# Causal mask of the key-on-partition scores in sixteen quarter-height passes, four side by side

## The chip, the cores and the metric

The kernel runs on one core of a Trainium2 chip. The metric is the device time of one execution in microseconds. Five engines work side by side on their own instruction lists: TensorE (matmuls, and a unit beside it that loads their weights), VectorE, ScalarE, GpSimd and SyncE, which issues most transfers. They wait for one another by semaphores.

## The reference

Two decoder layers over x of shape (32, 128, 128): 32 batches of 128 positions with 128 channels. Cut to the order of the parts:

```python
x = x + _L0_attn_ref(_layernorm(x), ...)           # 16 heads of 8, rotary
x = x + _L0_xattn_ref(_layernorm(x), ctx_768, ...) # 16 heads of 8, clipped
x = x + _L0_ffn_ref(_layernorm(x), ...)
x = x + _L1_attn_ref(_layernorm(x), ...)           # the causal one
x = x + _L1_xattn_ref(ctx_768, _layernorm(x), mask_BxS2_bk0, ...)
x = x + _L1_ffn_ref(_layernorm(x), ...)            # 8 experts, 2 per token
```

The part that the change touches is the causal attention of the second layer:

```python
att = jnp.einsum('bhqd,bhkd->bhqk', q, k) * scale
causal = jnp.tril(jnp.ones((Tx, Tx), dtype=bool))
att = jnp.where(causal[None, None], att, -jnp.inf)
att = jax.nn.softmax(att, axis=-1)
y = jnp.einsum('bhqk,bhkd->bhqd', att, v)
```

## The kernel before

The kernel is a row of phases, each a block of its own: self and cross attention of layer 0 in one block, a guard, the feed-forward of layer 0, the causal attention, the latent cross attention, the expert feed-forward. A phase starts when the one before it has ended. The attention phases all come from `attention` (line 225 on), which is called once for self and cross and once for the causal kind.

A phase works through 32 batches (n), in groups (G) of 4. P is 128, U is 4, GB is 4, GT is 512 (one bank of the accumulation memory). The 16 heads stand in 4 units (u) of 4 heads (j); a unit's 32 channels lie on partitions 32u to 32u + 31 (`rows_of`). PSUM is split by hand: `S` has two banks, `T` four, `OM` and `PB` one each.

For each batch scores are made twice. `scores` (lines 382 to 394) makes them with the query on the partition into `S`, two units at a time (`pair`), for the row maxima that VectorE takes (line 591, `maxes`). `key_scores` (from line 396) makes them again with the key on the partition into `T`, one bank per unit, in three rounds of four matmuls of 32 rows and 512 columns: high parts times high parts (line 408), then the query's low part (411), then the key's (413). `shift` (425) subtracts the maxima, ScalarE exponentiates (521), `weigh` (452) multiplies with the values and with ones.

In the causal kind `hide` (lines 370 to 380) first writes the mask into the banks by matmuls of constants: a slice of the mask table as weights and a slice of the identity, repeated for the 4 heads, as the moving operand. It takes two banks. Bank i uses partitions 64i to 64i + 63, so that two passes can run side by side, and each pass covers 64 of the 128 columns of each head, 4 x 64 = 256 columns. Two banks take 2 x 2 passes. `scores` calls it once per pair with table 0, `key_scores` twice with table 1, for banks 0 and 1 and for banks 2 and 3: 8 passes. The tables lie in the constants `const_r` (name `cr`), which are loaded at the start of the program (line 124) and copied by ScalarE (line 162).

What follows what on an engine is written out by hand in `ORDERS`. TensorE's list for the causal kind is "s0 k^5 T m y f0 s1 x^6 f1 w q^5 v^4". Iteration n runs the scores of batch n + 2 (s0, s1), the key scores of batch n (T), the transposed maxima of n + 1 (m), the output projection of n - 2 (y), the shift of n (f0, f1) and the weighing of n - 1 (w). A step with ^ runs once per group, so many batches before the group's first: the key projection k of a group stands between s0 and T, 5 iterations ahead.

Of the kernel before, what the change touches and what calls it, by code (L numbers as in the profile page):

```python
# [19 lines left out]
P = 128  # L20
# [4 lines left out]
GT = GB * P  # L25
E0 = 8
W_FFN0 = 3 * (E0 // 2 + 1) * P + E0
U = 4
# [35 lines left out]


C_ID, C_ONES, C_MASK = 0, P, 5 * P
C_PAIR = C_MASK + 4 * P
C_BEFORE = C_PAIR + (E0 // 2) * P
C_FULL = C_BEFORE + P
N_CONST_R = C_FULL + P  # L70
# [152 lines left out]
def attention(nc, phase, kinds, sb, bank, context=None, x_ready=None):  # L223
# [5 lines left out]
    def kind(n):  # L229
        return kinds[n // B]  # L230
# [16 lines left out]
    cr = sb["const_r"]  # L247
# [13 lines left out]
    S, T = bank[:, 0:2 * GT], bank[:, 2 * GT:6 * GT]  # L261
    OM, PB = bank[:, 6 * GT:7 * GT], bank[:, 7 * GT:8 * GT]

    def s_bank(u):
        return S[:, (u % 2) * GT:(u % 2 + 1) * GT].rearrange("p (j k) -> p j k", j=U)

    def t_bank(u):
        return T[:, u * GT:(u + 1) * GT]
# [35 lines left out]
    with ExitStack() as ctx:  # L304
# [48 lines left out]
        def rows_of(u):  # L353
            return slice(32 * u, 32 * u + 32)

        def batch_cols(n):
            return slice((n % GB) * P, (n % GB + 1) * P)
# [6 lines left out]
        def _(pe):  # L364
# [2 lines left out]
                pe.matmul(out, l[0], r[1], start=False, stop=False)  # L367
                return pe.matmul(out, l[1], r[0], start=False, stop=True)

            def hide(banks, c):  # L370

                half = P // 2
                for part in range(2):
                    at = C_MASK + (2 * c + part) * P
                    for i, out in enumerate(banks):
                        mine = slice(i * half, (i + 1) * half)
                        pe.matmul(out.rearrange("p (j q) -> p j q", j=U)[:, :, part * half:(part + 1) * half],
                                  cr[mine, at:at + P],
                                  cr[mine, C_ID + i * half:C_ID + (i + 1) * half].unsqueeze(1).broadcast_to([half, U, half]),
                                  start=part == 0, stop=False)  # L380

            def scores(n, pair):
                causal = kind(n) == "causal"
                if pair == 0:
                    pe.wait_ge(k_masked, n + 1)
                if 2 * n + pair > 0:
                    pe.wait_ge(max_done, 2 * n + pair)
                units = (2 * pair, 2 * pair + 1)
                if causal:
                    hide([S[:, u * GT:(u + 1) * GT] for u in range(2)], 0)  # L390
                for u in units:
                    mm = pe.matmul(s_bank(u), kq_hi[QUERY][(n // GB) % 2][rows_of(u), batch_cols(n)],  # L392
                                   k_hi_m[n % 2][rows_of(u), :, :], start=not causal, stop=True)
                mm.then_inc(scored, 1)

            def key_scores(n):
                causal, clip = kind(n) == "causal", kind(n) == "cross"
                pe.wait_ge(q_masked, 2 * n + 2)
                if n > 0:
                    pe.wait_ge(exp_done, 2 * n)  # L400
                g = (n // GB) % 2
                k_hi, k_lo, q_hi, q_lo = kq_hi[KEY][g], kq_lo[KEY][g], q_hi_m[n % 2], q_lo_m[n % 2]
                if causal:
                    for u in (0, 2):
                        hide([t_bank(u), t_bank(u + 1)], 1)
                out = [t_bank(u).rearrange("p (j q) -> p j q", j=U) for u in range(U)]
                for u in range(U):
                    pe.matmul(out[u], k_hi[rows_of(u), batch_cols(n)], q_hi[rows_of(u), :, :],
                              start=not causal, stop=False)
                for u in range(U):  # L410
                    pe.matmul(out[u], k_hi[rows_of(u), batch_cols(n)], q_lo[rows_of(u), :, :], start=False, stop=False)
                for u in range(U):
                    mm = pe.matmul(out[u], k_lo[rows_of(u), batch_cols(n)], q_hi[rows_of(u), :, :],  # L413
                                   start=False, stop=clip)
                    if clip and u % 2 == 1:
                        mm.then_inc(keyed, 1)
# [78 lines left out]
            for step, i in steps("PE"):  # L495
                if step == "T":
                    key_scores(i)
                elif step in ("f0", "f1"):
                    shift(i, int(step[1]))
                elif step == "y":  # L500
                    out_project(i)
                elif step in ("s0", "s1"):
                    scores(i, int(step[1]))
                elif step == "m":
                    transpose_max(i)
                elif step == "w":
                    weigh(i)
                elif step == "x":
                    transpose_x(i)
                elif step == "c":  # L510
                    transpose_c(i)
                else:
                    project(step, i)
# [362 lines left out]
def gated_experts(nc, phase, sb, ps, ready):  # L876
# [12 lines left out]
    with ExitStack() as ctx:  # L889
# [59 lines left out]
        def _(pe):  # L949
# [22 lines left out]
            def spread_gate(it, n, k):  # L972
                if k == 0:
                    pe.wait_ge(g_done, it * 2 + (n + 1))
                if (NB - 1) * n + k > 0:
                    pe.wait_ge(gate_copied, it * (2 * NB - 2) + ((NB - 1) * n + k))
                sel = cr[0:2 * E0, C_PAIR + k * P:C_PAIR + (k + 1) * P]
                pe.matmul(GATE[:, :], sel, g_parts[n % 2][:, :], start=True, stop=True).then_inc(gate_spread, 1)
# [1326 lines left out]
def shape_constants():  # L2305

    c = np.zeros((P, N_CONST), np.float32)
    eye = np.eye(P, dtype=np.float32)
    c[:, C_ID:C_ID + P] = eye
    for u in range(U):  # L2310
        c[32 * u:32 * u + 32, C_ONES + u * P:C_ONES + (u + 1) * P] = 1.0
        for g in range(U):
            c[32 * u + g, C_DIAG + g] = 1.0
            c[32 * u + DH * g:32 * u + DH * (g + 1), C_SLOT + g] = 1.0
    e = np.arange(E0)
    c[:, C_EARLIER:C_EARLIER + E0 * E0] = (e[None, :] < e[:, None]).astype(np.float32).reshape(1, -1)
    for h in range(2):
        c[h * P // 2:(h + 1) * P // 2, C_HEAD + h] = 1.0
    c[:, C_BEFORE:C_BEFORE + P] = np.triu(np.ones((P, P), np.float32), 1)
    c[:, C_FULL:C_FULL + P] = 1.0  # L2320
    c[:, C_DESCEND:C_DESCEND + E1] = E1 - np.arange(E1)
    c[:, C_FILL:C_FILL + MOST] = TT * np.arange(MOST)
    c[:, C_REGION:C_REGION + E1] = B * P * np.arange(E1)
    c[:, C_TILE:C_TILE + N_TILES] = np.arange(N_TILES)
    c[:, C_TILE_ROW:C_TILE_ROW + N_TILES] = TT * np.arange(N_TILES) - B * P
    c[:, C_HOME:C_HOME + 2 * B] = P * np.arange(2 * B)[None, :] + np.arange(P)[:, None]
    for k in range(E0 // 2):
        c[[2 * k, E0 + 2 * k], C_PAIR + k * P:C_PAIR + k * P + P // 2] = 1.0
        c[[2 * k + 1, E0 + 2 * k + 1], C_PAIR + k * P + P // 2:C_PAIR + (k + 1) * P] = 1.0
    hidden = np.triu(np.ones((P, P), np.float32), 1) * np.float32(MASKED)  # L2330
    for n, table in enumerate((hidden.T, hidden)):
        for half in range(2):
            rows = table[half * P // 2:(half + 1) * P // 2]
            at = C_MASK + (2 * n + half) * P
            c[0:P // 2, at:at + P] = rows
            c[P // 2:P, at:at + P] = rows
    rate = (np.float32(1.0) / np.float32(10000.0) ** (np.arange(0, DH, 2, dtype=np.float32) / np.float32(DH)))
    ch = np.arange(D)

    angle = (rate[ch % (DH // 2)][:, None] * np.arange(P, dtype=np.float32)[None, :]).astype(np.float32)  # L2340
    sign = np.where(ch % DH < DH // 2, -1, 1).astype(np.float32)[:, None]
    c[:, C_ROPE:C_ROPE + P] = np.cos(angle)
    c[:, C_ROPE + P:C_ROPE + 2 * P] = sign * np.sin(angle)

    angle = (rate[ch % DH // 2] * (ch // DH).astype(np.float32)).astype(np.float32)
    sign = np.where(ch % 2 == 0, -1, 1).astype(np.float32)
    for n, table in enumerate((np.cos(angle), sign * np.sin(angle))):
        c[:, C_TURN + n * P:C_TURN + (n + 1) * P] = table[None, :]
        c[:, C_TURN_COL + n] = table
    return c  # L2350


def packed(i):
# [36 lines left out]
    def experts(routed, shared):  # L2390
# [13 lines left out]
        "cols": np.stack(cols, 1),  # L2404
        "rows": np.concatenate([rows_of(r) for r in rows], 1),
        "consts": shape_constants(),
    }

# [15 lines left out]
```

## Time and profile before

| | |
|---|---|
| median of 3 runs | 1434.62 us (1428.91 to 1439.69) |
| the profiled execution | 1435.96 us |
| its span | 1434.2 us |
| granted TensorE clock, mean | 0.912 |
| TensorE matmuls busy | 1197.7 us (84%) |
| VectorE, ScalarE, GpSimd busy | 878.1, 674.8, 768.1 us |
| mask passes (line 377) | 512, from 715.8 to 957.0 us |

The span is the time from the first to the last instruction of the profiled execution; the time has a little around it. Times of rows are in us from the start of the span unless marked ns. PE is TensorE's matmuls, PEld its weight loads, DVE VectorE, ACT ScalarE, POOL GpSimd. Matmuls are pipelined: a row's length holds its latency, so what a round costs is read from the starts of two rounds.

### The profile page before, as it was taken

To read this page: it belongs to the slowest core of one execution; us is meant where nothing else is said; L and a number is where in the kernel's file an instruction comes from. 1 tells how busy PE (TensorE), PEld (TensorE's weight loads), DVE (VectorE), ACT (ScalarE), POOL (GpSimd) and SP (SyncE) were. 2 spreads that over 40 slices of the span, in tenths; PEclk is the share of its full clock that TensorE was granted. 3 is DMA by queue.
4 is the path that set the end of the run, shared out by engine and by line. 5 is a ranking of instruction groups with operands and counts; after the bars stand their busy time and mean duration, and the time that the engine had idled before them with its cause. 6 is when DMAs were issued, how large, how long until landed. Compare 5 with 4: busy or idle time off the path is not lost. (4 is left out here: it accounts for less than half of the span.)

```text
span 1434.2 us, 33962 instructions
## 1 busy us (share of the span) xinstructions
PE 1197.7 (84%) x12478; PEld 901.5 (63%) x12478; DVE 878.1 (61%) x2007; ACT 674.8 (47%) x1298; POOL 768.1 (54%) x870
## 2 busy tenths in 40 slices
PE   1899998788888874999799999984999993199992
PEld 0577775555555563666467777764899983088881
DVE  3688876599999955666255666555888843122223
ACT  1345444344545422455345545437888631055551
POOL 3777873555666511444455555525776757344452
PEclk9999998799999985999789999996999955599996
DMA  9910000000000000000000000000000001256656
GB/s 346 380 56 10 2 2 15 14 15 15 14 15 7 2 2 1 1 1 0 1 2 2 2 2 3 2 2 23 12 13 2 20 25 52 78 192 201 196 192 179
DMA packets 58863, 75.27 MB, mean 52 GB/s; under 512 B 13246, under 2 KB 40003, under 8 KB 58576
## 3 DMA queue, kind: packets, MB, share of 16 engines
q1 hardware_dynamic: 53328, 63.59, 13.8%
q0 software_dynamic: 4544, 8.47, 1.7%
q8 instruction: 101, 1.65, 0.5%
q10 hardware_dynamic: 832, 1.09, 0.2%
q14 instruction: 58, 0.48, 0.1%
HBM read 40.24 MB, written 31.70 MB: 50 GB/s over the span
## 5 line engine op out<-in xcount | busy, mean ns | idle before, releaser
L591 DVE TENSOR_REDUCE maxes<-bank 128x8 f32<-128x1024 f32 x192 | 234.4, 1221 | 56.6 <-PE bank L392 55.1
L521 ACT ACTIVATE self_probs<-bank 128x1024 f32<-128x1024 f32 x128 | 129.1, 1022 | 46.1 <-PE bank L425 45.7
L1429 POOL DMA_INDIRECT returned<-relu_y,relu_slots x78 | 76.7, 984 | 93.8 <-DVE relu_y L1404 81.3
L1372 ACT ACTIVATE relu_hidden<-bank,cols 128x256 f32<-128x256 f32 x156 | 74.0, 474 | 94.0 <-PE bank L1330 80.5
L528 ACT ACTIVATE self_neg_max<-bank 128x512 fp32r<-128x512 f32 x64 | 38.2, 597 | 149.9 <-PE bank L439 149.9
L732 POOL TENSOR_TENSOR self_k_hi_m<-self_kq_hi,const 128x512 fp32r<-128x512 f32 x64 | 66.6, 1041 | 78.4 <-ACT self_kq_hi L549 78.4
L1330 PE MATMUL bank<-relu_s,relu_w_tile 128*128 128x256 f32 x312 | 94.3, 385 | 0.5 <-DVE relu_s L1398 0.5
L1338 PE MATMUL bank<-relu_hidden,relu_w_tile 128*128 128x256 f32 x312 | 92.5, 379 | 0.0
L1398 DVE COPY relu_s<-bank 128x256 f32<-128x256 f32 x39 | 16.6, 425 | 110.5 <-issue 81.1
L597 DVE TENSOR_SCALAR bank<-bank 128x1024 f32<-128x1024 f32 x64 | 78.2, 1223 | 3.3 <-PE bank L413 3.3
L601 DVE RECIPROCAL self_recip<-bank 128x128 f32<-128x128 f32 x64 | 61.2, 957 | 30.2 <-PE bank L452 28.2
L2215 POOL DMA_INDIRECT routed<-latent_rows,latent_place_i x64 | 63.0, 984 | 30.8 <-issue 16.6
L732 POOL TENSOR_TENSOR causal_q_lo_m<-causal_kq_lo,const 128x512 fp32r<-128x512 f32 x32 | 33.3, 1041 | 84.5 <-PE bank L425 84.4
L452 PE MATMUL bank<-self_probs,values 128*32 128x128 f32 x2048 | 73.1, 286 | 1.4 <-ACT self_neg_max L528 1.2
L452 PE MATMUL bank<-self_probs,head_ones 128*32 128x128 f32 x2048 | 70.8, 280 | 0.0
L425 PE MATMUL bank<-self_neg_max,const_r 32*128 32x512 f32 x256 | 62.0, 475 | 9.7 <-DVE bank L597 6.3
L521 ACT ACTIVATE causal_probs<-bank 128x1024 f32<-128x1024 f32 x64 | 64.5, 1022 | 5.2 <-PE bank L425 2.7
L732 POOL TENSOR_TENSOR self_q_lo_m<-self_kq_lo,const 128x512 fp32r<-128x512 f32 x64 | 66.7, 1042 | 0.3 <-PE bank L425 0.2
L732 POOL TENSOR_TENSOR self_q_hi_m<-self_kq_hi,const 128x512 fp32r<-128x512 f32 x64 | 66.6, 1041 | 0.0
L452 PEld LDWEIGHTS bank<-self_probs,values 128*32 128x32 f32 x2048 | 54.9, 113 | 18.6 <-issue 15.9
L439 PE MATMUL bank<-ident,maxes 128*128 128x128 f32 x384 | 65.2, 294 | 0.5 <-POOL maxes L755 0.3
L1338 PEld LDWEIGHTS bank<-relu_hidden,relu_w_tile 128*128 128x128 f32 x312 | 59.3, 190 | 8.3 <-ACT relu_hidden L1372 0.2
(380 smaller groups left out, 3434.9 us busy)
## 6 DMA issues: line engine op xcount, KB each, us to landing
relu_w_tile<-in_w_ffn SPq DMA_DIRECT2D x39, 512.0 KB
routed<-blank SPq DMA_DIRECT2D x1, 19760.0 KB, 60.9
relu_slots<-routed SPq DMA_DIRECT2D x39, 130.0 KB
relu_back<-returned SPq DMA_DIRECT2D x16, 256.0 KB, 4.4
x_all<-in_x SPq DMA_DIRECT2D x8, 256.0 KB, 8.2
x_before<-x_all SPq DMA_DIRECT2D x8, 256.0 KB, 2.7
out_x<-x_all SPq DMA_DIRECT2D x8, 256.0 KB, 4.0
self_ctx_in<-in_ctx SPq DMA_DIRECT2D x8, 192.0 KB, 2.6
```

Of the source, the lines that this page charges most:

```text
L425: mm = pe.matmul(t_bank(u), cr[rows_of(u), C_ONES + u * P:C_ONES + (u + 1) * P], neg_max[n % 2][rows_of(u), :], start=False, stop=True, sk ...
L439: mm = pe.transpose(OM[:, j * P:(j + 1) * P], maxes[n % 2][:, j * P:(j + 1) * P], sb["ident"][:, :])
L452: mm = pe.matmul(OM[rows_of(u), c:c + P], of(u, j), probs[n % 2][:, u, j, :], start=j == 0, stop=j == U - 1)
L521: act.activation(probs[n % 2][:, 2 * pair:2 * pair + 2, :, :].rearrange("p u j q -> p (u j q)"), T[:, 2 * pair * GT:(2 * pair + 2) * GT], ...
L591: dve.tensor_reduce(out.rearrange("p j u -> p u j"), S.rearrange("p (u j k) -> p u j k", u=2, j=U), AX.X, ALU.max, negate=True).then_inc(m ...
L597: dve.tensor_scalar(t, t, CLAMP / scale, -CLAMP / scale, ALU.min, ALU.max).then_inc(clipped, 1)
L732: pool.tensor_tensor(out[n % 2][:, :, :], src[(n // GB) % 2][:, batch_cols(n)].bitcast(F32).unsqueeze(1).broadcast_to([P, U, P]), slots.un ...
L1330: pe.matmul(HT[i % 2][:, 0:TT], w_tile[t % NW][:, c * P:(c + 1) * P], s[t % 2][:, :], start=True, stop=True)\
L1338: pe.matmul(YT[t % 2][:, 0:TT], w_tile[t % NW][:, F1 + c * P:F1 + (c + 1) * P], hidden[i % C1][:, :], start=c == 0, stop=c == C1 - 1).then ...
L1372: act.activation(hidden[i % C1][:, :], HT[i % 2][:, 0:TT], ACT.Relu, bias=sb["cols"][:, bass.ds(r + (COL_RELU + c), 1)]).then_inc(hidden_d ...
L1429: pool.indirect_dma_start(returned[:, :], bass.IndirectOffsetOnAxis(ap=slots[t % NX][:, b, P:P + 1].bitcast(I32), axis=0), y[t % NY][:, b, ...
L2215: pool.indirect_dma_start(routed[:, :], bass.IndirectOffsetOnAxis(ap=place_i[u % 3][:, k, b:b + 1], axis=0), rows[G % 4][:, k, n % GB, :], ...
```

## The change

`hide` takes a list of banks of any length and the place of the table, and splits partitions and columns by the number of banks. `scores` calls it as before, with two banks. `key_scores` calls it once with all four banks of `T`: 4 x 4 = 16 passes of 32 rows and 4 x 32 = 128 columns, bank i on partitions 32i to 32i + 31. The table of the key scores gets four parts instead of two, each repeated on four groups of partitions, so the constants grow by 2 x 128 columns.

```diff
-C_PAIR = C_MASK + 4 * P
+C_PAIR = C_MASK + 6 * P
...
-            def hide(banks, c):
-
-                half = P // 2
-                for part in range(2):
-                    at = C_MASK + (2 * c + part) * P
+            def hide(banks, mask):
+
+                share = P // len(banks)
+                for part in range(len(banks)):
+                    at = mask + part * P
                     for i, out in enumerate(banks):
-                        mine = slice(i * half, (i + 1) * half)
-                        pe.matmul(out.rearrange("p (j q) -> p j q", j=U)[:, :, part * half:(part + 1) * half],
+                        mine = slice(i * share, (i + 1) * share)
+                        pe.matmul(out.rearrange("p (j q) -> p j q", j=U)[:, :, part * share:(part + 1) * share],
                                   cr[mine, at:at + P],
-                                  cr[mine, C_ID + i * half:C_ID + (i + 1) * half].unsqueeze(1).broadcast_to([half, U, half]),
-                                  start=part == 0, stop=False)
+                                  cr[mine, C_ID + i * share:C_ID + (i + 1) * share].unsqueeze(1)
+                                  .broadcast_to([share, U, share]), start=part == 0, stop=False)
...
-                    hide([S[:, u * GT:(u + 1) * GT] for u in range(2)], 0)
+                    hide([S[:, u * GT:(u + 1) * GT] for u in range(2)], C_MASK)
...
-                    for u in (0, 2):
-                        hide([t_bank(u), t_bank(u + 1)], 1)
+                    hide([t_bank(u) for u in range(U)], C_MASK + 2 * P)
...
-    for n, table in enumerate((hidden.T, hidden)):
-        for half in range(2):
-            rows = table[half * P // 2:(half + 1) * P // 2]
-            at = C_MASK + (2 * n + half) * P
-            c[0:P // 2, at:at + P] = rows
-            c[P // 2:P, at:at + P] = rows
+    at = C_MASK
+    for table, parts in ((hidden.T, 2), (hidden, 4)):
+        share = P // parts
+        for part in range(parts):
+            for i in range(parts):
+                c[i * share:(i + 1) * share, at:at + P] = table[part * share:(part + 1) * share]
+            at += P
```

On TensorE, an iteration with a key projection between scores and mask. Before (outputs are named with the partition count of the bank, x8 is the number of passes in a row):

```order
L377 MATMUL bank<-const_r 128x4x64 x4
L392 MATMUL bank<-causal_k_hi_m,causal_kq_hi 128x512 x2
L366 MATMUL bank<-causal_x_hi,w_hi 128x512
L367 MATMUL bank<-causal_x_lo,w_hi 128x512
L368 MATMUL bank<-causal_x_hi,w_lo 128x512
L377 MATMUL bank<-const_r 128x4x64 x8
L408 MATMUL bank<-causal_q_hi_m,causal_kq_hi 128x512 x4
L411 MATMUL bank<-causal_q_lo_m,causal_kq_hi 128x512 x4
L413 MATMUL bank<-causal_q_hi_m,causal_kq_lo 128x512 x4
L439 MATMUL bank<-ident,maxes 128x128 x4
```

The same place of the changed kernel, whose lines behind `hide` stand one higher:

```order
L377 MATMUL bank<-const_r 128x4x64 x4
L392 MATMUL bank<-causal_k_hi_m,causal_kq_hi 128x512 x2
L366 MATMUL bank<-causal_x_hi,w_hi 128x512
L367 MATMUL bank<-causal_x_lo,w_hi 128x512
L368 MATMUL bank<-causal_x_hi,w_lo 128x512
L377 MATMUL bank<-const_r 128x4x32 x16
L407 MATMUL bank<-causal_q_hi_m,causal_kq_hi 128x512 x4
L410 MATMUL bank<-causal_q_lo_m,causal_kq_hi 128x512 x4
L412 MATMUL bank<-causal_q_hi_m,causal_kq_lo 128x512 x4
L438 MATMUL bank<-ident,maxes 128x128 x4
```

On TensorE again, an iteration without a key projection, from the weighing of the iteration before on. Before:

```order
L452 MATMUL bank<-causal_probs,head_ones 32x128 x16
L377 MATMUL bank<-const_r 128x4x64 x4
L392 MATMUL bank<-causal_k_hi_m,causal_kq_hi 128x512 x2
L377 MATMUL bank<-const_r 128x4x64 x8
L408 MATMUL bank<-causal_q_hi_m,causal_kq_hi 128x512 x4
L411 MATMUL bank<-causal_q_lo_m,causal_kq_hi 128x512 x4
L413 MATMUL bank<-causal_q_hi_m,causal_kq_lo 128x512 x4
L439 MATMUL bank<-ident,maxes 128x128 x4
```

The same place of the changed kernel:

```order
L451 MATMUL bank<-causal_probs,head_ones 32x128 x16
L377 MATMUL bank<-const_r 128x4x64 x4
L392 MATMUL bank<-causal_k_hi_m,causal_kq_hi 128x512 x2
L377 MATMUL bank<-const_r 128x4x32 x16
L407 MATMUL bank<-causal_q_hi_m,causal_kq_hi 128x512 x4
L410 MATMUL bank<-causal_q_lo_m,causal_kq_hi 128x512 x4
L412 MATMUL bank<-causal_q_hi_m,causal_kq_lo 128x512 x4
L438 MATMUL bank<-ident,maxes 128x128 x4
```

Nothing changes places in either; the 8 passes ahead of the first key-score round have become 16. In the second place the mask stands right behind the scores of line 392, in the first behind the key projection (lines 366 to 368).

## Rows read from the trace of the kernel before

**Rows 1.** Stretches: length, busy PE, PEld, DVE, ACT, POOL, granted clock, DMA share, GB/s
```profile
727.00:966.00 239.00, 235.38 (x3509) 165.53 (x3508) 138.63 (x238) 112.16 (x152) 125.92 (x134) 1.00 0.01 2
966.00:1000.00 34.00, 14.48 (x60) 12.24 (x61) 16.31 (x76) 24.56 (x57) 18.04 (x35) 0.60 0.10 24
```

**Rows 2.** Waits of PE from 727 to 966 us: us in total, times, longest
```profile
PE bank L465 <- DVE causal_o_t L605: 1.4, 1, 1.4
...
PE bank L377 <- ACT causal_probs L521: 0.2, 1, 0.2
```

**Rows 3.** Timeline of PE, one batch: start, length, line, rows*weight columns, moving operand, count
```profile
849.25 0.50 PE L392 MATMUL bank<-causal_k_hi_m,causal_kq_hi 32*128 32x512 f32 x2
849.68 0.74 PE L377 MATMUL bank<-const_r 64*128 64x256 f32 x8
850.35 0.51 PE L408 MATMUL bank<-causal_q_hi_m,causal_kq_hi 32*128 32x512 f32 x4
850.68 0.41 PE L411 MATMUL bank<-causal_q_lo_m,causal_kq_hi 32*128 32x512 f32 x4
850.91 0.42 PE L413 MATMUL bank<-causal_q_hi_m,causal_kq_lo 32*128 32x512 f32 x4
```

**Rows 4.** Timeline of PEld, same batch; then the group, 740 to 955 us
```profile
849.68 0.54 PEld L377 LDWEIGHTS bank<-const_r 64*128 64x128 f32 x8 [0.24 <-issue]
...
850.46 0.20 PEld L411 LDWEIGHTS bank<-causal_q_lo_m,causal_kq_hi 32*128 32x128 f32 x4
850.69 0.20 PEld L413 LDWEIGHTS bank<-causal_q_hi_m,causal_kq_lo 32*128 32x128 f32 x4
...
L377 PEld LDWEIGHTS bank<-const_r 64*128 64x128 f32 x456 | 32.2, 185 | 20.4 <-issue 18.7 <-POOL causal_q_hi_m L732 1.2
```

**Rows 5.** Timeline of PE, further on in the same iteration
```profile
852.50 0.50 PE L377 MATMUL bank<-const_r 64*128 64x256 f32 x4
852.93 0.49 PE L392 MATMUL bank<-causal_k_hi_m,causal_kq_hi 32*128 32x512 f32 x2
853.26 0.40 PE L425 MATMUL bank<-causal_neg_max,const_r 32*128 32x512 f32 x2
853.59 1.08 PE L452 MATMUL bank<-causal_probs,values 128*32 128x128 f32 x32
854.49 1.06 PE L452 MATMUL bank<-causal_probs,head_ones 128*32 128x128 f32 x32
```

**Rows 6.** Timeline of PE, latent attention: full height, 128 and 256 columns
```profile
1061.91 0.22 PE L1724 MATMUL bank<-latent_mask_rows,const_r 128*128 128x128 f32 x1
1061.97 0.34 PE L1722 MATMUL bank<-latent_k_hi,latent_q_hi 128*128 128x256 f32 x1
1062.14 0.22 PE L1724 MATMUL bank<-latent_mask_rows,const_r 128*128 128x128 f32 x1
```

**Rows 7.** Timeline of PE, value projection: full height, 128 columns
```profile
856.53 0.27 PE L366 MATMUL bank<-w_hi,causal_x_hi 128*128 128x128 f32 x1
856.64 0.27 PE L367 MATMUL bank<-w_lo,causal_x_hi 128*128 128x128 f32 x1
```

**Rows 8.** Timeline of PE, a batch with the key projection ahead of the mask
```profile
842.13 0.74 PE L377 MATMUL bank<-const_r 64*128 64x256 f32 x8
...
843.14 0.40 PE L411 MATMUL bank<-causal_q_lo_m,causal_kq_hi 32*128 32x512 f32 x4
```

**Rows 9.** Page, part 2 (GB/s in 40 slices), and timeline of the start
```profile
GB/s 346 380 56 10 2 2 15 14 15 15 14 15 7 2 2 1 1 1 0 1 2 2 2 2 3 2 2 23 12 13 2 20 25 52 78 192 201 196 192 179
...
7.09 1.80 ACT L162 ACTIVATE const_r<-staged_consts 128x1920 fp32r<-128x1920 f32 x1 [2.36 <-DMA staged_consts<-in_consts]
...
13.05 0.29 DVE L178 TENSOR_TENSOR staged_weights<-staged_weights,const 128x128 f32<-128x128 f32 x1 [13.05 <-DMA w_out<-in_weights]
```

**Rows 10.** Timeline of ACT and DVE, the batch of rows 3
```profile
847.59 1.02 ACT L521 ACTIVATE causal_probs<-bank 128x1024 f32<-128x1024 f32 x1
...
849.79 1.23 DVE L591 TENSOR_REDUCE maxes<-bank 128x8 f32<-128x1024 f32 x1 [0.45 <-PE bank L392]
```

## Prediction

> **What bounds the kernel now.** I read the busy time by stretch first, then the waits of the stage that the change touches, then its order of time, one batch at a time. The causal attention's steady part runs from about 727 to 966 us [rows 1]: TensorE's matmuls are busy 235.38 of 239.00 us there at a granted clock of 1.00 (2.4 GHz), while VectorE has 138.63, ScalarE 112.16 and GpSimd 125.92. After 966 the stage is over and the clock at 0.60. TensorE hardly waits for anybody: the longest wait in those 239 us is 1.4 us, once [rows 2]. So this stage lasts as long as TensorE's own list, and what is cut from the list comes off the end as long as nothing else turns up as a wait.
>
> But busy does not mean streaming. In one batch [rows 3] the two score matmuls of 512 columns start at 849.25 and the eight mask passes only at 849.68, 0.43 us later; the first key scores start at 850.35 and the second round at 850.68, 0.33 later; the third comes 0.23 behind that. All three are rounds of 512 columns that differ in what stands around them. 0.23 is the price where the weights come ahead: the loads of the second and third rounds start while the round before still streams (850.46 against 850.68, 850.69 against 850.91) [rows 3, 4]. 0.33 is that and 0.10 for a first load that nobody could take ahead. 0.43 is that and another 0.10, in which the array runs empty before the next load may start: the mask's loads begin at 849.68 with 0.24 us of idle load unit before them, put down to issue and to no engine [rows 4]. What distinguishes 0.43 is that the number of rows changes, 32 to 64 [rows 3]. Where 32 rows follow 32 rows, at 852.93 and 853.26, the step is 0.33 and no drain shows [rows 5]. So a change between full, half and quarter height costs about 0.10 of drain and 0.10 of exposed load: 0.20 us.
>
> Could it be another shape that costs, and not another height? Then the quarter-height mask of 128 columns would still drain ahead of and behind the key scores of 512, and nothing would be gained. The nearest rows are full-height neighbours of 256, 128 and 256 columns, which follow one another without a drain, 0.06 and 0.17 us apart [rows 6]; so I take the height. By the height the sum is -11.0 us, by the shape it is 0.
>
> On this the Trainium skill has a rule, in TensorEngine Tiling (Array Packing), Key Properties: going to another tiling mode drains the array, going to another tile of the same mode does not. By that rule the sum is the one by the height.
>
> **The change, part by part.** Every causal batch runs the mask before its key scores once, 32 batches.
>
> 1. *Passes.* Before: 8 passes of 64 rows and 256 columns, in 4 rounds of two side by side. After: 16 passes of 32 rows and 128 columns, in 4 rounds of four. Streaming halves. But a round also loads 128 weight columns per pass, and these loads are as long as before. The eight loads of the old block take 0.54 us as a group, and the mean of one is 0.185, so three steps from round to round take 0.355 and one 0.118 [rows 4]. Two full-height neighbours with 128 columns and 128 weight columns go at 0.11 [rows 7]. A stream of 128 columns whose weights are there takes only 0.06: 1061.91 to 1061.97 [rows 6]. So a new round is bound by its load: 0.11 at the least. I take 0.118, as the new block's loads start at the same point as the old, once the last matmul of their row group has begun. Halving the columns is worth nothing by itself; four rounds stay four rounds.
>
> 2. *Will four loads at once hold that pace?* The old block had two. Four quarter-height loads stand ahead of every key-score round, and the round at 850.35 costs the same 0.33 with four loads exposed [rows 3] as the one at 852.93 with two [rows 5]: the loads run side by side. The issue of 16 pairs of load and matmul is bounded by the weighing, where 32 pairs take 0.90 us, 853.59 to 854.49 [rows 5], so 16 take 0.45. Four rounds at 0.118 are 0.47, just above it. The mask operands are constants, so no new wait comes with the extra passes.
>
> 3. *Height changes.* The mask now has the height of the key scores behind it and, mostly, of the scores ahead of it.
>  - Scores right ahead: before, scores to second key round is 850.68 - 849.25 = 1.43 us [rows 3]. After: 0.33 (as from the first to the second key round, its own load exposed), four rounds 0.47, then the first key round with weights loaded ahead, 0.23. Together 1.03, so 0.40 saved.
>  - Something of full height ahead (key projection or weighing): before, mask to second key round is 843.14 - 842.13 = 1.01 [rows 8]. After: 0.22 for the first round with its load exposed (0.10 + 0.118), two rounds 0.24, one more step 0.12 to the key scores, 0.23. Together 0.81, so 0.20 saved.
>  By the list of orders the key projection of groups 2 to 7 stands between scores and mask (6 batches), and the last 2 batches have no scores two batches on. In 1 more, the second, the mask waits 0.2 us for the exponential [rows 2], so only 0.20 is saved. So 23 x 0.40 + 9 x 0.20 = 9.2 + 1.8 = 11.0 us. With rounds of 0.11 it would be 32 x 4 x 0.008 = 1.0 more.
>
> 4. *The scores' own mask* (two banks, half height, 4 passes per pair) stays, with its changes of height.
>
> 5. *The constants* grow from 1920 to 2176 columns, 128 KB more. At the first slice's 346 GB/s [rows 9] that is 0.37 us. VectorE's first work waits for loads until 13.05 us [rows 9] and the first projection hangs on it, so I count it in full; the lower end is 0. ScalarE's copy of 1.80 us ends at 8.89 [rows 9] and grows by 256/1920 of that, 0.24 us; ScalarE is idle until its first normalisation, so that costs nothing, and would cost 0.24 if it did.
>
> 6. *Who becomes late next.* The second score mask must wait for VectorE's maximum of the first: that ends at 849.79 + 1.23 = 851.02, the mask starts at 852.50 [rows 5, 10]. Of these 1.48 us at most 0.42 go. The key mask waits for the exponential that ends at 847.59 + 1.02 = 848.61 [rows 10] and starts at 849.68, 1.07 later; nothing between them gets shorter. So TensorE remains the bound.
>
> Sum: -11.0 + 0.4 = -10.6 us. Against the profiled execution (span 1434.2, time 1435.96) that gives 1425.4 us; its time is 1.3 above the median of 1434.62, and from the median the sum gives **1424.0 us**, 0.7% less.
>
> **Rivals.**
> - *Weights don't come ahead in quarter rounds* (chance 0.12). Then a round is load plus stream, 0.118 + 0.057. Adds 0.057 x 4 x 32 = 7.3 us: 1431.3. For it: no row shows rounds this short at quarter height with 128 weight columns. Against it: the key rounds load the same four row groups during the stream before [rows 4]. The Trainium skill, TensorE: Matmul & The Clock Gate, Part 3, says that a load overlaps running matmuls only where its row group is another one, which taken strictly is this rival; the loads at 850.46 and 850.69 go against it.
> - *Slower: the four loads queue for one path* (0.03). 4 x 0.11 = 0.44 per round, (0.44 - 0.118) x 4 x 32 = 41 us more: 1465. It decides from a round of 0.118 + 10.6 / 128 = 0.20 us on. Against it: 0.33 with four loads and with two, as above.
> - *No gain* (0.08): the drains stay because they hang on the shape, or VectorE's maxima, the GpSimd masks or the exponentials become the bound: 1434 to 1436. For it: these engines are 47 to 58% busy in long pieces of 1.0 to 1.2 us. Against it: the neighbours without a drain [rows 6] and the slack of 1.07 and 1.48 us.
> - *More than counted* (0.07): rounds of 0.11 and a stage end that falls better with the clock, which goes to 0.60 in the 34 us behind the stage [rows 1]; a stretch at the lower level costs up to half of its length. About 1419.
>
> **How the numbers follow.** The forecast has 0.70, its own range being 1420 to 1428: the sum within a microsecond or so, and the spread of single runs, which here go from 1428.91 to 1439.69. The range from 1416 to 1432 takes in the load rival and most of the case of more than counted. About 1% is what a measurement of this kernel can tell from no change, and faster by over 1% means below 1420.3. The forecast reaches there by its spread in about 2 of 9 cases (0.15), more than counted mostly (0.05), together 0.20. Slower by over 1% is the queue rival, 0.03, and a little of the third, 0.04 in all. The rest, 0.76, is within 1%.
>
> **What the new profile would show.** Scores to mask 0.33 instead of 0.43; mask to key scores about 0.47 instead of 0.67; first to second key round 0.23 instead of 0.33; the load unit's idle pieces ahead of the key mask gone in 23 batches; the stage near 11 us shorter with TensorE as full as now. If mask to key scores is 0.70, the first rival holds; if it is over 1 us, the second. If these steps are right and the stage isn't shorter, a wait of TensorE for another engine must have come up. The sum is wrong in its height changes if mask to key scores still shows idle load time ahead of the key round.

## The result

The changed kernel takes 1425.26 us in the median of 8 executions (1420.62 to 1430.07), the kernel before 1435.54 in 8 (1428.91 to 1445.33): a ratio of 0.9925, interval 0.9907 to 0.9944. That is 10.3 us less, by the interval 8 to 13. Forecast were 10.6 less from a median of 1434.62, so 1424.0 us.

From the page of the changed kernel, span and the first row of part 1:

```profile
span 1420.8 us, 34474 instructions
...
PE 1192.8 (84%) x12734; PEld 904.7 (64%) x12734; DVE 877.0 (62%) x2007; ACT 675.0 (48%) x1298; POOL 767.3 (54%) x870
```

The counts say that 256 more matmuls run, each with its load: 16 instead of 8 passes in 32 batches. TensorE is busy for 1192.8 us instead of 1197.7, which is no measure of the gain.

The steady part of the causal attention, busy time by stretch (columns as in [rows 1]), and TensorE's waits in it:

```profile
727.00:955.00 228.00, 225.59 (x3714) 164.79 (x3712) 138.36 (x236) 113.95 (x155) 126.67 (x135) 0.99 0.01 2
```

```profile
PE bank L377 <- DVE maxes L590: 0.5, 1, 0.5
```

TensorE is as full as before (225.59 of 228.00 us), VectorE, ScalarE and GpSimd do the same work in less time, and TensorE's longest wait is 0.5 us. No other engine has taken over.

How long the stage is I read from the first to the last start of the mask passes, with the clock's lower level for the first 11 us of it in both. Before:

```profile
L377 PE MATMUL bank<-const_r x512: 271/278/579, 715.8 to 957.0; 64*128 64x256 f32 x171
```

After:

```profile
L377 PE MATMUL bank<-const_r x768: 216/273/579, 720.2 to 949.8; 32*128 32x128 f32 x128, 64*128 64x256 f32 x64
```

241.2 us before, 229.6 after: 11.6 less. From the first normalisation of the stage (`causal_mean_var`) to that of the next it is 268.7 and 257.1, the same 11.6. The stage's period is sharper still, as nothing but TensorE sets it. The transposes of x run once per group of four batches; starts of two neighbours before and after:

```profile
776.13 0.66 PE L472 MATMUL bank<-ident,causal_xn 128*128 128x128 f32 x4
...
806.80 0.66 PE L472 MATMUL bank<-ident,causal_xn 128*128 128x128 f32 x4
```

```profile
777.88 0.65 PE L471 MATMUL bank<-ident,causal_xn 128*128 128x128 f32 x4
...
807.04 0.66 PE L471 MATMUL bank<-ident,causal_xn 128*128 128x128 f32 x4
```

30.67 us before, 29.16 after, and the same to 0.03 for the five such pairs of a trace that lie at full clock. The two at the stage's start, where the clock is low and not every step runs yet, are shorter. The change takes 1.51 us off four batches.

**One batch after**, scores right ahead of the mask (columns as in [rows 3]):

```profile
760.27 0.49 PE L392 MATMUL bank<-causal_k_hi_m,causal_kq_hi 32*128 32x512 f32 x2
760.29 0.77 PE L377 MATMUL bank<-const_r 32*128 32x128 f32 x14
760.78 0.45 PE L407 MATMUL bank<-causal_q_hi_m,causal_kq_hi 32*128 32x512 f32 x2
760.89 0.27 PE L377 MATMUL bank<-const_r 32*128 32x128 f32 x2
761.00 0.44 PE L407 MATMUL bank<-causal_q_hi_m,causal_kq_hi 32*128 32x512 f32 x2
761.07 0.61 PE L410 MATMUL bank<-causal_q_lo_m,causal_kq_hi 32*128 32x512 f32 x4
...
761.84 0.33 PE L438 MATMUL bank<-ident,maxes 128*128 128x128 f32 x1
```

and of the load unit:

```profile
760.29 0.62 PEld L377 LDWEIGHTS bank<-const_r 32*128 32x128 f32 x14
...
761.84 0.20 PEld L438 LDWEIGHTS bank<-ident,maxes 128*128 128x128 f32 x2 [0.36 <-issue]
```

The mask starts 0.01 to 0.02 us behind the scores, not 0.33: the two row groups that the scores of this pair leave idle begin their passes at once. From there on the row groups run apart, two ahead, two behind: mask passes (760.89) come after the first key scores of other row groups (760.78). The loads of the mask begin at 760.29 too, beside the scores, and run on to 760.91. The end is the transposed maximum at 761.84, with 0.36 us of idle load unit ahead of it, the change back to full height. From the scores to it: 1.57 us. Before, the scores of [rows 3] at 849.25 were followed by

```profile
851.26 0.55 PE L439 MATMUL bank<-ident,maxes 128*128 128x128 f32 x3
```

2.01 us. So 0.44 saved.

**A batch with the key projection ahead**, after:

```profile
753.37 0.67 PE L377 MATMUL bank<-const_r 32*128 32x128 f32 x16
753.87 0.46 PE L407 MATMUL bank<-causal_q_hi_m,causal_kq_hi 32*128 32x512 f32 x4
754.15 0.41 PE L410 MATMUL bank<-causal_q_lo_m,causal_kq_hi 32*128 32x512 f32 x4
...
754.73 0.33 PE L438 MATMUL bank<-ident,maxes 128*128 128x128 f32 x1
```

1.36 us from mask to transposed maximum. Before, the mask of [rows 8] at 842.13 was followed by

```profile
843.70 0.55 PE L439 MATMUL bank<-ident,maxes 128*128 128x128 f32 x3
```

1.57 us, so 0.21 saved. Three of the one and one of the other make 1.53; the period gives 1.51. Of the 32 batches of the trace 23 are of the first kind, and in just these the load unit's idle time ahead of the key mask is gone; 9 are of the second kind, as counted.

### The profile page after: what moved, and what is told of

It is laid out like the page before. It is cut to its first block and busy times, and to the rows that moved or that the text cites. A ratio compares the mean times of both kernels' runs of the same rounds, so it can differ in the third digit from the quotient of the medians.

```text
span 1420.8 us, 34474 instructions
## 1 busy us (share of the span) xinstructions
PE 1192.8 (84%) x12734; PEld 904.7 (64%) x12734; DVE 877.0 (62%) x2007; ACT 675.0 (48%) x1298; POOL 767.3 (54%) x870
```

## Experiments

All periods below are read from the starts of the transposes as above; "stage" is the time from the first to the last mask pass. Kernels without a ratio ran once, so their whole time says little; period and stage are what they are read by.

| kernel | period of 4 batches, us | stage, us | whole kernel against before |
|---|---|---|---|
| before | 30.67 | 241.2 | |
| changed | 29.16 | 229.7 | 0.9925 (0.9907 to 0.9944) |
| changed, again | 29.16 | 229.7 | 0.9933 (0.9903 to 0.9964) |
| a_wide | 29.23 | 230.4 | |
| b_narrow | 32.12 | 252.9 | |
| c_by_bank | 29.59 | 232.9 | |
| e_same | 29.57 | 232.8 | |
| e_height | 30.79 | 242.2 | |
| v_second | 27.53 | 220.4 | 0.9895 (0.9822 to 0.9968) |
| v_second again | 27.53 | 220.4 | 0.9881 (0.9834 to 0.9928) |
| v_both | 27.57 | 227.8 | 0.9920 (0.9895 to 0.9946) |
| v_late | 27.53 | 218.3 | 0.9869 (0.9835 to 0.9903) |

### Is it the streaming or the height? (a_wide, b_narrow)

a_wide keeps quarter height and makes each pass 256 columns wide again:

```diff
+                for part in range(4):
+                    at, half, shift = mask + part * P, part // 2 * 64, (1 - part % 2) * 32
...
+                        pe.matmul(out.rearrange("p (j q) -> p j q", j=U)[:, :, half:half + 64],
+                                  cr[mine, at:at + P],
+                                  cr[mine, C_WIDE + shift:C_WIDE + shift + 64].unsqueeze(1)
+                                  .broadcast_to([32, U, 64]), start=part == 0, stop=False)
```

> The changed kernel with passes of quarter height that are 256 columns wide again (16 passes, four side by side, a moving operand padded with zeros, same result). Read by the time from the first to the last mask pass, 241.2 us before and 229.6 us after the change. Theory (the gain is the removed changes of height, a round is bound by its weight load of 0.11 to 0.12 us): a stream of 256 columns takes 0.11 and hides behind the load, so 229 to 231 us. Rival (the gain is the halved streaming): all of it is lost, about 241 us.

Mask and key scores of a batch with the key projection ahead:

```profile
845.93 0.75 PE L388 MATMUL bank<-const_r 32*128 32x256 f32 x16
846.52 0.40 PE L418 MATMUL bank<-causal_q_hi_m,causal_kq_hi 32*128 32x512 f32 x4
846.74 0.40 PE L421 MATMUL bank<-causal_q_lo_m,causal_kq_hi 32*128 32x512 f32 x4
```

The stage takes 230.4 us, the period is 29.23 instead of 29.16. Twice the columns cost 0.07 us per four batches. So the halved streaming is worth next to nothing, as expected.

b_narrow is the other half: the kernel before, its half-height passes 128 columns wide and twice as many.

```diff
-                    for u in (0, 2):
-                        hide([t_bank(u), t_bank(u + 1)], 1)
+                    for u in (0, 2):
+                        hide_narrow([t_bank(u), t_bank(u + 1)], 1)
```

with, in `hide_narrow`, parts of 32 columns per head and `cr[mine, q:q + 32]` as the moving operand.

> The kernel before with its half-height mask of the key scores in passes of 128 columns: 16 passes, two side by side, 8 rounds; each pass streams half as much, the heights and their changes stay. Theory (a round costs its weight load, however few columns it streams): 4 more rounds of 0.11 to 0.118 us in 32 batches, 14 to 15 us more than the kernel before: 255 to 256 us from first to last mask pass. Rival (rounds cost their streaming): 8 rounds of half the columns cost what 4 did, 241 us.

```profile
853.84 1.11 PE L389 MATMUL bank<-const_r 64*128 64x128 f32 x16
854.87 0.50 PE L420 MATMUL bank<-causal_q_hi_m,causal_kq_hi 32*128 32x512 f32 x4
```

1.03 us from mask to key scores instead of 0.67, the stage 252.9 instead of 241.2, 11.7 more. The rival had it at 241. The expectation of 14 to 15 more was somewhat high: the four further rounds cost 0.36 together, 0.09 each. Taken one by one the later rounds start 0.11 us apart (six steps from 854.00 to 854.67), the price of a load. The rest of the difference stands in the first step, 0.17 us where the kernel before has 0.23 (849.68 to 849.90): its stream is half as long. The two runs together leave the removed changes of height, and what they let the row groups do, as what the change gains by.

### The price of a change of height by itself (e_same, e_height)

Both add one pass with zero weights between mask and key scores, in every batch; e_same on 32 rows, e_height on 64:

```diff
+                    pe.matmul(T[:, 0:P], cr[0:P // 2, C_WIDE:C_WIDE + P], cr[0:P // 2, C_ID:C_ID + P],
+                              start=False, stop=False)
```

(`P // 4` in e_same.)

> The changed kernel with one more pass between mask and key scores: quarter height, 128 columns, zero weights, into bank 0 (adds zero). It has the height of its neighbours. Both theories: one load-bound round more on row group 0 in 32 batches, 0.118 x 32 = 3.8 us, so 233.5 us from first to last mask pass (229.7 without it).

> The same extra pass at half height (64 rows, same columns, zero weights), so that the height changes twice between mask and key scores. Theory of the height: drain 0.10, load 0.11, stream 0.06, drain 0.10, and the key round's load 0.11 exposed, about 0.47 us in each of 32 batches: 15 us, 244.5 us from first to last mask pass, 11 us above the run with the quarter-height pass. Rival (what costs is another shape of the moving operand or the number of passes, not the height): the same 233.5 us as that run.

e_same, a batch with the key projection ahead:

```profile
848.53 0.67 PE L378 MATMUL bank<-const_r 32*128 32x128 f32 x16
849.03 0.27 PE L406 MATMUL bank<-const_r 32*128 32x128 f32 x1
849.04 0.55 PE L410 MATMUL bank<-causal_q_hi_m,causal_kq_hi 32*128 32x512 f32 x4
849.32 0.50 PE L413 MATMUL bank<-causal_q_lo_m,causal_kq_hi 32*128 32x512 f32 x4
```

e_height, the same place:

```profile
853.03 0.67 PE L378 MATMUL bank<-const_r 32*128 32x128 f32 x16
853.63 0.32 PE L406 MATMUL bank<-const_r 64*128 64x128 f32 x1
853.88 0.51 PE L410 MATMUL bank<-causal_q_hi_m,causal_kq_hi 32*128 32x512 f32 x4
854.22 0.41 PE L413 MATMUL bank<-causal_q_lo_m,causal_kq_hi 32*128 32x512 f32 x4
```

From mask to the second key round it is 0.79 us with the quarter-height pass and 1.19 with the half-height one. Per batch, from the periods, the quarter-height pass costs (29.57 - 29.16) / 4 = 0.10 us and the half-height pass (30.79 - 29.16) / 4 = 0.41. The 0.30 between them are two changes of height at the same place, with the same columns and weights. That is 0.15 per change, drain and exposed load together, somewhat less than the 0.20 of the prediction. One thing comes with the height: in e_same three of the four key scores start beside the extra pass (849.04), in e_height none can, so the 0.15 holds this loss too. The stages are 232.8 us, where 233.5 had been expected, and 242.2, where the theory of the height had 244.5 and the rival 233.5. One pass of the wrong height in a batch takes back the whole gain of the change (0.41 against 0.38 us per batch).

### How far the row groups run apart (c_by_bank)

```diff
+                for i, out in enumerate(banks):
+                    for part in range(4):
```

instead of parts outside and banks inside.

> The changed kernel with the 16 passes in another order: all four parts of bank 0 (row group 0), then of bank 1, and so on, instead of part by part over the banks. Same passes, same result. If matmuls start strictly in program order, the row groups work one after another: 16 steps of about 0.118 us instead of 4, 1.42 us more in each of 32 batches, some 45 us more, 275 us from first to last mask pass. If a row group goes ahead of a waiting one (as the passes of the idle row groups seem to do right behind the scores in the trace after), the time stays near 229.6 us.

```profile
852.40 0.50 PE L401 MATMUL bank<-causal_k_hi_m,causal_kq_hi 32*128 32x512 f32 x2
852.74 0.58 PE L386 MATMUL bank<-const_r 32*128 32x128 f32 x13
853.13 0.44 PE L416 MATMUL bank<-causal_q_hi_m,causal_kq_hi 32*128 32x512 f32 x1
853.13 0.30 PE L386 MATMUL bank<-const_r 32*128 32x128 f32 x3
853.25 0.47 PE L416 MATMUL bank<-causal_q_hi_m,causal_kq_hi 32*128 32x512 f32 x3
```

The stage is 232.9 us: 3.2 more, not 45. So a matmul does not wait for earlier ones of another row group to finish; in a batch with the key projection ahead the block costs the same 0.50 us in either order:

```profile
845.48 0.70 PE L386 MATMUL bank<-const_r 32*128 32x128 f32 x16
845.98 0.48 PE L416 MATMUL bank<-causal_q_hi_m,causal_kq_hi 32*128 32x512 f32 x4
...
846.86 0.33 PE L447 MATMUL bank<-ident,maxes 128*128 128x128 f32 x1
```

But going ahead has an end. Behind the scores the mask begins 0.34 us later, not 0.01. In the order by parts the idle row groups' first passes stand third and fourth in the list, here ninth and thirteenth, and they don't start early. The place in the list alone doesn't explain it. In the batch with the key projection ahead, the window 845.48 to 845.60 shows four passes, one for each row group:

```profile
845.48 0.36 PE L386 MATMUL bank<-const_r 32*128 32x128 f32 x4
```

All four start by 845.52, and the others only from 845.65 on. So the first pass of row group 3, the thirteenth in the list, goes ahead of nine that wait. What differs behind the scores is that row group 0 has four passes waiting behind a running matmul, and not three. Whether that is the limit wasn't tried.

The run also says how much of the gain hangs on the order. From scores to transposed maximum it is now 1.71 us (the scores of 852.40, and below), against 1.57 by parts and 2.01 before:

```profile
854.11 0.33 PE L447 MATMUL bank<-ident,maxes 128*128 128x128 f32 x1
```

So 0.30 of the 0.44 us come with the equal height in this order too, and 0.14 only when the passes are listed by parts. With the key projection ahead it is 1.38 against 1.36. Three of 0.14 and one of 0.02 make 0.44, and the periods differ by 0.43. The loads fit: by parts loads of mask passes go on beside the scores (from 760.29), by banks a single one is taken ahead (852.51) and the next starts at 852.74.

### Further versions (v_second, v_both, v_late)

v_second makes the mask of the second pair of scores in quarter height too, on row groups 2 and 3, between the two halves of the shift:

```diff
-                    hide([S[:, u * GT:(u + 1) * GT] for u in range(2)], C_MASK)
+                    if pair:
+                        hide_quarter([S[:, u * GT:(u + 1) * GT] for u in range(2)], C_MASK + 6 * P, 2)
+                    else:
+                        hide([S[:, u * GT:(u + 1) * GT] for u in range(2)], C_MASK)
```

> A version that goes further: the mask of the second pair of scores is also made in quarter-height passes (2 banks, 4 rounds of two, on row groups 2 and 3), while the first pair keeps half height. Between the first half of the shift (row groups 0 and 1) and the second half there is then no change of height. Before, these steps are 0.43 + 0.43 + 0.33 = 1.19 us. If a row group can go ahead while others stream, the mask rounds run beside the shift and the whole takes about 0.79 us: 0.40 less in 31 batches, 12 us, 217 us from first to last mask pass and about 1413 us. If the mask waits for the shift's streams, 0.33 + 0.47 + 0.23 = 1.03: 5 us less, 225 us and 1420 us.

```profile
845.65 0.50 PE L437 MATMUL bank<-causal_neg_max,const_r 32*128 32x512 f32 x2
845.66 0.66 PE L387 MATMUL bank<-const_r 32*128 32x128 f32 x8
846.16 0.45 PE L405 MATMUL bank<-causal_k_hi_m,causal_kq_hi 32*128 32x512 f32 x2
846.44 0.41 PE L437 MATMUL bank<-causal_neg_max,const_r 32*128 32x512 f32 x2
```

From shift through mask and scores to the second half of the shift: 0.79 us instead of 1.19 (852.07 to 853.26 before), the mask starting 0.01 behind the shift. The period falls by 1.63 us to 27.53, which is 0.41 per batch. But the stage took 220.4 us, not 217, and the whole kernel 0.9895, hardly below the changed kernel and with a wide interval. What the stage lacks stands at its start. The stretches at the lower level there (columns as in [rows 1], the granted clock third from last), first the changed kernel's, then v_second's:

```profile
706.90:730.80 23.90, 16.10 (x57) 10.57 (x57) 7.10 (x17) 8.57 (x17) 13.75 (x17) 0.50 0.00 0
```

```profile
712.80:743.50 30.70, 23.04 (x108) 15.48 (x109) 10.71 (x27) 9.50 (x18) 16.19 (x20) 0.50 0.00 1
```

The clock is at 0.50, its lower level (1.2 GHz), and before and behind them at 1.00. The stretch begins 0.9 to 1.3 us behind the stage's first normalisation in every profile. In the profile before, both of the changed kernel and those of a_wide, b_narrow, c_by_bank, e_same and e_height, the lower level at the stage's start lasted 23.9 us. In v_second it lasted 30.7. The form of the key mask is not what moves it, as it is the same before and after the change.

In the whole kernel more is in play than the stage. In the profiled execution of v_second the feed-forward ahead of the stage, whose code is the same, took 183.0 us, in that of the changed kernel 175.6.

v_both uses `hide_quarter` for both pairs.

> Quarter-height mask for both pairs of scores. The second pair gains as in v_second (0.40 us per batch, 12 us less than the changed kernel without the clock's share). The first pair stands behind work of full height: its mask takes 4 rounds instead of 2 (0.57 to the scores instead of 0.43), but the scores' load comes ahead (0.23 instead of 0.33 behind them): +0.03 us per batch if the key mask starts as before, 1 us more than v_second, 218 us from first to last mask pass. If the key mask of row groups 2 and 3 goes ahead beside the first pair's mask, it is even with v_second or up to 0.2 us per batch better (6 us), 211 us.

> The changed kernel once more, unchanged, on the same chip as v_both and in turns with the kernel before: 229.7 us from first to last mask pass if the clock stands as in its first profile, ratio 0.9925 within its interval.

The changed kernel gave 229.7 us and a ratio of 0.9933 again. v_both has the same period as v_second, 27.57, so the first pair neither gains nor loses; the overlap hoped for there is not to be seen. And its clock rose later still, after 47.8 us:

```profile
714.90:762.70 47.80, 39.91 (x280) 29.67 (x282) 16.48 (x36) 18.01 (x30) 26.20 (x31) 0.50 0.00 1
```

Its stage took 227.8 us and the kernel 0.9920, the same as the changed kernel. 218 or 211 us had been expected for the stage: most of what the shorter period brings is given back by the clock at the start.

v_late is v_second with the old form for the scores of the first four batches:

```diff
-                    if pair:
+                    if pair and n > 3:
```

> v_second with the scores' masks of the first four batches in the form of the changed kernel (half height), so that the start of the stage, where TensorE's clock still stands at its lower level, has the same work as in the changed kernel. In the first profile of v_second the lower level lasted 30.7 us there, in v_both 47.8, in the changed kernel 23.9 both times. If the new form of the masks at the start is what holds the clock down, the lower level lasts 23.9 us again and the time from first to last mask pass is 229.7 - 28 x 0.41 = 218.2 us, some 11.5 us below the changed kernel: about 1414 us, ratio 0.984. If the length of that stretch is chance, it varies here too, and v_late and v_second are alike. The period of four batches is 27.5 us in either case.

> v_second unchanged, in turns with v_late. If the masks' form holds the clock down: the lower level at the start of the stage lasts about 30 us again and the kernel is 2 to 4 us slower than v_late. If it is chance: the same time as v_late within the spread of single runs.

v_late's stretch at the lower level:

```profile
706.00:729.90 23.90, 16.31 (x57) 10.61 (x57) 7.11 (x17) 8.78 (x17) 13.63 (x16) 0.50 0.00 0
```

The lower level lasted 23.9 us again, and the stage took 218.3 us where 218.2 had been expected. v_second's lasted 30.7 again, its stage 220.4 again. So the length of that stretch repeats with the form of the first masks and is not chance. Why TensorE's clock comes later with quarter-height masks there isn't settled: the passes there are more, shorter and less high, and no run separates these. In whole kernels v_late is the fastest measured, 1422.17 us in the median of 6 against 1440.77 before, ratio 0.9869; 0.984 had been expected. It is 1.6 us below v_second in turns with it, where 2 to 4 had been expected; the intervals overlap, and only the stage tells the two apart.

## Why the prediction was right, point by point

- **TensorE's list sets the stage.** Held: 225.59 of 228.00 us busy, longest wait 0.5 us. What was cut from the list came off the stage.
- **Halving the columns is worth nothing.** Held, by a_wide (streams twice as long cost 0.07 us per four batches) and b_narrow (half the stream in each of twice as many rounds, 11.7 us more).
- **Four loads at once hold the pace.** Held: mask to key scores is 0.50 us with full-height work ahead. The rival of the four queuing loads wanted over 1 us. Nor is there a round of load plus stream, which would make it 0.70. Rounds start 0.11 us apart (753.54, 753.65, 753.76, 753.87), a little less than the 0.118 of the sum.
- **Height changes, scores ahead.** The size held, the path didn't. The sum had scores to mask 0.33, mask to key scores 0.47, first to second key round 0.23, together 1.03 and 0.40 saved. Measured were 0.01, 0.49 and 0.29, where the last two no longer are rounds of all four row groups: two run ahead, two behind. The sum took the row groups as going in step. In the causal stage before nothing else was to be seen, since the mask had another height than its neighbours; but self attention has one place where key scores stand right behind scores, and the two on idle row groups start with the scores, ahead of the two listed first (258.76; the window is 258.40 to 258.70):

```profile
258.43 0.50 PE L392 MATMUL bank<-self_k_hi_m,self_kq_hi 32*128 32x512 f32 x2
258.43 0.49 PE L408 MATMUL bank<-self_q_hi_m,self_kq_hi 32*128 32x512 f32 x2
```

 Up to the transposed maximum the row groups behind set the time, and they do wait for the scores: mask at 760.61, key scores at 761.00, second round at 761.28, steps of 0.34, 0.39 and 0.28, together 1.01 where the sum had 1.03. So 0.44 came out. That it is so near 0.40 is in part luck: had the passes been listed by banks it would have been 0.30 (c_by_bank), and the sum doesn't ask for the order.
- **Height changes, full height ahead.** 0.20 forecast, 0.21 measured. Its parts stand elsewhere than forecast: mask to key scores 0.50 instead of 0.58, first to second key round 0.28 instead of 0.23, together 0.78 instead of 0.81. In a_wide they are 0.59 and 0.22. Behind a narrow pass the key scores' row starts 0.06 us behind its load (753.87 and 753.81), in a_wide 0.12 (846.52 and 846.40). If a load takes the 0.11 of a round, some 0.05 of it are still to come in the first case, and 0.23 + 0.05 is the 0.28. This is an estimate from the rows; it would only shift time from one row to the next, and the sum is right.
- **Sum of the stage.** 11.0 forecast, 11.6 measured. The numbers of batches, 23 and 9, held; with the two savings as measured they give 23 x 0.44 + 9 x 0.21 = 12.0.
- **The whole kernel.** 10.6 forecast, 10.3 measured, with an interval of 8 to 13: that the two are 0.3 apart is luck, the 11.6 of the stage is what carries the forecast.
- **The constants.** 0.37 us was counted, and nothing came. VectorE's first instruction and ScalarE's copy after:

```profile
7.07 2.02 ACT L162 ACTIVATE const_r<-staged_consts 128x2176 fp32r<-128x2176 f32 x1 [2.66 <-DMA staged_consts<-in_consts]
...
13.01 0.29 DVE L178 TENSOR_TENSOR staged_weights<-staged_weights,const 128x128 f32<-128x128 f32 x1 [13.01 <-DMA w_out<-in_weights]
```

 13.01 instead of 13.05, the copy 0.22 us longer (0.24 forecast) and hidden. The wait ends with `w_out`, which another queue issues behind other loads; 128 KB more in the first load do not hold it up.
- **Who becomes late next.** Nobody, with 0.42 less per batch; and with another 0.41 less in v_late TensorE's longest single wait was 1.4 us.

In the profiled pair the spans differ by 13.4 us (1434.2 and 1420.8), not 11.6. That is 11.6 in the causal stage, 4.3 against it up to the end of cross attention, 6.3 for it in the latent attention and 0.3 against it in the feed-forwards, whose code is the same in both. In the self attention the clock rose later in the profile after: the two-bank score round of line 392 is 0.48 us long before (at 57.36) and 0.63 after (at 57.30).

Over the twelve profiles of this case it rose either at 52 to 58 us (six, before among them) or at 71 to 73 (six, the changed kernel's both among them; v_second has one of each), so this follows no change. The latent attention took from 273.7 to 283.7 us over the profiles of this case. The feed-forward ahead of the causal stage took 175.6 to 176.3 us in five profiles (before, both of the changed kernel, b_narrow, v_late), with the clock at its lower level for 41 to 44 us of it, and 182.3 to 183.0 in the other seven, with 58 to 61 us; its code is the same in all. All three are part of what makes single executions of one kernel 10 us apart.

## What to carry to other kernels

Ahead of counting columns, look at what separates neighbouring blocks on TensorE: at full clock a change between full, half and quarter height costs 0.15 to 0.20 us (the array empties and the next load is exposed), more than a round of passes at 0.11. Bring small constant passes (masks, biases) to the height of their neighbours, even at more passes, as long as the rounds don't grow by more than the changes are worth, and let the list alternate over the row groups, so that idle ones can start while the others still stream: in this kernel that order is a third of the gain behind the scores (0.14 of 0.44 us). Read such a change from the period of the loop at constant clock: it is good to 0.03 us where whole executions differ by 10, and look separately at the stage's start, where another form of the first passes moved the clock's rise by 7 and by 24 us (v_second, v_both).

## What the runs showed of the hardware that I had not expected

- Matmuls of quarter height go ahead of earlier ones of other row groups: mask passes began 0.01 us behind scores (or shift) that still streamed 0.3 us on two other row groups. Listed by banks (c_by_bank) they did not go ahead there, while the thirteenth pass of the list went ahead of nine waiting ones where no scores stood before them.
- The clock's lower level at the start of the stage lasted 23.9 us in nine profiles of eight kernels with half-height masks of the scores there, 30.7 in both of v_second and 47.8 in the one of v_both.
